# Flamingo gated block on one core: first batch's parts copied inside SBUF, masks written by VectorE, one transpose per kind and batch

## The reference

```
x = x + tanh(g_xattn) * xattn(layernorm(x), ctx)
x = x + tanh(g_ffn)   * moe(layernorm(x))

xattn: 16 heads of 8 channels
  y  = softmax(causal(q k^T / sqrt(8))) v          # self, q, k, v from x
  y += softmax(qc kc^T / sqrt(8)) vc               # cross, qc from x, kc, vc from ctx
  return y Wp + bp
moe: sigmoid router over 16 experts, best 2 of 4 groups, best 4 experts,
     out = sum_e combine[:, e] * (silu(x Wg_e) * (x Wu_e)) Wd_e
```

## Time and profile before

| what | value |
|---|---|
| median of three runs | 349.49 us |
| span of the profiled execution | 347.6 us |
| TensorE busy | 318.1 us (92%) |
| VectorE busy | 256.4 us (74%) |
| ScalarE busy | 196.2 us (56%) |
| GpSimd busy | 151.1 us (43%) |
| DMA, mean | 116 GB/s |
| bytes moved | 40.45 MB |

### The profile page before, as it was taken

One profiled execution on the slowest core, in us unless ns is written; L12 is line 12 of the kernel. 1 busy time (PEld: TensorE's weight loads), 2 busy tenths in 40 slices (PEclk: granted clock), 3 DMA queues, 4 the chain that ended last, 5 costly groups with the idle time before them and its releaser, 6 DMA issues.

```text
span 347.6 us, 8679 instructions
## 1 busy us (share of the span) xinstructions
PE 318.1 (92%) x3186; PEld 247.7 (71%) x3186; DVE 256.4 (74%) x639; ACT 196.2 (56%) x399; POOL 151.1 (43%) x176
## 2 busy tenths in 40 slices
PE   1579599989999999999999999999999999978696
PEld 0455365666687788778887888787888787856665
DVE  4238666868898888988798888888889854748742
ACT  2433356767667765687637765675666467532041
POOL 3884061404470588047633494318410722903422
PEclk9856759999999999999999999999999999989999
DMA  4269674688563855537655365077156005214000
GB/s 123 68 183 188 146 194 115 145 209 187 199 151 103 184 131 149 143 96 151 147 139 133 88 172 140 20 152 183 34 124 141 0 18 90 37 50 88 16 1 15
DMA packets 32889, 40.45 MB, mean 116 GB/s; under 512 B 3440, under 2 KB 29824, under 8 KB 30368
## 3 DMA queue, kind: packets, MB, share of 16 engines
q1 hardware_dynamic: 32004, 38.46, 46.7%
q10 hardware_dynamic: 844, 1.45, 1.7%
HBM read 29.84 MB, written 7.45 MB: 107 GB/s over the span
## 4 chain that ended last, share of the span: by engine, by line
PE 76%; DVE 7%; DMA 6%; SPq 5%; POOL 2%; issue 2%; ACT 1%; POOLq 0%; DVEq 0%
PE bank L918 15%; PE bank L846 14%; PE bank L825 8%; PE bank L943 7%; PE bank L800 7%; PE bank L803 6%; PE bank L822 5%; DMA k_stack<-tri_k 4%; SPq L427 2%; PE bank L893 2%; DVE row_max L1011 2%; PE bank L861 2%; PE bank L852 2%; SPq L426 1%; PE bank L956 1%
## 5 line engine op out<-in xcount | busy, mean ns | idle before, releaser
L1011 DVE TENSOR_REDUCE row_max<-bank 128x2 f32<-128x512 f32 (+1 forms) x224 | 146.9, 686 | 43.0 <-PE bank L803 24.9
L709 ACT ACTIVATE probs<-bank 128x512 f32<-128x512 f32 x224 | 127.5, 595 | 57.5 <-PE bank L825 27.7
L918 PE MATMUL bank<-xn2T,w_pairs_sb 128*128 128x256 f32 x256 | 68.0, 392 | 1.5 <-issue 0.9
L846 PE MATMUL bank<-probs,v_ext 128*32 128x256 f32 (+1 forms) x1024 | 57.2, 365 | 0.0
L626 POOL TENSOR_TENSOR f_h<-f_h,comb 128x512 f32<-128x512 f32 x32 | 40.3, 1273 | 36.1 <-DMA comb<-c_scr 20.4
L803 PE MATMUL bank<-k_stack,q_stack 72*128 72x256 bf16 x256 | 49.9, 284 | 2.7 <-DVE row_max L1011 2.1
L918 PEld LDWEIGHTS bank<-xn2T,w_pairs_sb 128*128 128x128 f32 x256 | 44.7, 193 | 8.3 <-issue 2.8
L825 PE MATMUL bank<-q_stack,k_stack 73*128 73x256 bf16 x256 | 49.2, 284 | 1.0 <-DMA q_stack<-shiftT 0.9
L412 POOL TENSOR_TENSOR rest<-proj,part 128x512 f32<-128x512 f32 x14 | 16.2, 1160 | 74.7 <-ACT part L682 74.6
L846 PEld LDWEIGHTS bank<-probs,v_ext 128*32 128x32 f32 x1024 | 30.0, 112 | 19.9 <-issue 4.7
L800 PE MATMUL bank<-k_stack,q_stack 121*128 121x128 bf16 (+1 forms) x384 | 39.1, 231 | 2.4 <-DMA k_stack<-tri_k 1.9
(11 more groups left out here) (113 smaller groups left out, 367.9 us busy)
## 6 DMA issues: line engine op xcount, KB each, us to landing
k_stack<-k_scr SPq DMA_DIRECT2D x45, 192.0 KB
q_stack<-q_scr SPq DMA_DIRECT2D x14, 576.0 KB
comb<-c_scr SPq DMA_DIRECT2D x14, 512.0 KB, 6.7
q_scr<-part SPq DMA_DIRECT2D x46, 64.0 KB
k_scr<-part SPq DMA_DIRECT2D x46, 64.0 KB
x_in<-in_x SPq DMA_DIRECT2D x8, 128.0 KB, 2.4
w_pairs_sb<-in_w_pairs SPq DMA_DIRECT2D x1, 1024.0 KB, 7.8
out<-y_out SPq DMA_DIRECT2D x8, 128.0 KB, 1.9
```

What stands on the lines that cost most here:

```text
L709: nc.scalar.activation(probs[:, seq % NP, :], exp_bank[s % 2][:, :], ACT.Exp).then_inc(exp_done, 1)
L846: last = pe.matmul(pv_bank[32 * n:32 * n + VW, col + q0:col + T], v[:, VW // 2 * odd:VW // 2 * odd + VW], weights, start=odd == 0 and kt = ...
L918: last = pe.matmul(bank_of[:, n * T:(n + 1) * T], w[:, e0:e0 + 128], xn2T[:, :], start=True, stop=True)
L1011: nc.vector.tensor_reduce(row_max[:, kind, qt, h0:h0 + nh], max_bank[k % 2][:, :].rearrange("p (h k) -> p h k", h=nh), AX.X, ALU.max).then ...
```

## The change

Batch 0 no longer goes through device memory. `copy_first` copies each part from SBUF into the stacks, 8 partitions of destination at a time: for each of the 2 kinds and 3 parts, three DMAs for q on SyncE's queue (`fq`) and three for k on ScalarE's (`fk`), 36 in all. ScalarE writes part 0 of batch 0 straight from PSUM, without `proj` (the query weights are multiplied by the scale once, beforehand, by VectorE), and VectorE takes the remainders of both kinds from PSUM (`first_rest`); GpSimd splits nothing of batch 0. The mask tiles are made at partitions 64 to 127 by GpSimd ahead of the first `rstd` (`masks:0`), with the shift row in them, and VectorE copies them into the stacks of all three slots (`tri`, six copies of 64 x 4096 bf16), two ahead of the splits of batch 0 and four ahead of the first reduction. The maxima and the router's weights are laid out so that one transpose gives all 256 tokens (rows are then heads times 2); the last batch's combT stays as it was. The waits for x and for the context are separate.

```diff
 'act':
-        xnT_e:0 proj_e:0 part0:0 pd0:0 proj_e:0:1 v_e:0 part0:0:1 qh:0 pd0:0:1 xnT_e:1 proj_e:1 part0:1 qh:0:1
-        proj_e:1:1 qst:0:1 part0:1:1 v_e:1 xnT_e:2 proj_e:2:1 sh_e:0 proj_e:2 sh_e:0:2 exp_e:0 exp_e:0:1 part0:2
+        xnT_e:0 proj_e:0 fk:0 proj_e:0:1 fk:0:1 fk:0:2 v_e:0 fk:0:3 fk:0:4 fk:0:5 xnT_e:1 proj_e:1 part0:1
+        proj_e:1:1 part0:1:1 v_e:1 xnT_e:2 proj_e:2:1 sh_e:0 proj_e:2 sh_e:0:2 exp_e:0 exp_e:0:1 part0:2
 'dve':
-        stats1:0 xnv:0 scale:0 stats1:1 sp1:0 sp3:0 stats1:2 tmax:0 ...
+        stats1:0 xnv:0 scale:0 gate:0 stats1:1 tri:0 tri:0:1 sp1:0 sp3:0 sp1:0:1 sp3:0:1 stats1:2 tri:0:2 tri:0:3 tri:0:4 tri:0:5 tmax:0 ...
 'pool':
-        rstd1:0 more:0 xres:0 rstd1:1 vclear:0 xn1:1 sp1:0:1 sp3:0:1 rstd1:2 ...
+        masks:0 rstd1:0 rows:0 xres:0 rstd1:1 xn1:1 vclear:0 rstd1:2 ...
 'sp':
-        load:0 w:0 load:1 load:2 ones:0 pd1:0 pd2:0 load:3 kh:0 pd1:0:1 pd2:0:1 kh:0:1 pd0:1 kst:0:1 tri:0 shd:0 pd2:1
-        pd1:1 pd1:1:1 pd0:1:1 pd2:1:1 shd:0:2 qst:1 kst:1 qst:1:1 shd:0:1 pd2:2 kst:1:1 tri:0:1 pd1:2 pd0:2 pd1:2:1
+        load:0 w:0 load:1 load:2 ones:0 fq:0 fq:0:1 fq:0:2 load:3 fq:0:3 fq:0:4 fq:0:5 pd0:1 pd2:1 pd1:1 shd:0
+        pd1:1:1 pd0:1:1 pd2:1:1 shd:0:2 qst:1 kst:1 qst:1:1 shd:0:1 pd2:2 kst:1:1 pd1:2 pd0:2 pd1:2:1
...
+        def first_rest(eng, kind):
+            src = (gate_bank, up_bank)[kind]
+            for at, bias in ((0, bias_q[:, 1 - kind:2 - kind]), (T, cols_sb[:, 3 - kind:4 - kind])):
+                last = eng.scalar_tensor_tensor(out=rest[:, kind, at:at + T], in0=src[:, at:at + T], scalar=bias,
+                                                in1=part[:, kind, 0, at:at + T], op0=ALU.add, op1=ALU.subtract)
+            last.then_inc(rest_done[kind], 1)
...
+        def copy_first(eng, qk, kind, n):
+            eng.wait_ge(split[kind], n + 1)
+            if kind == SELF:
+                eng.wait_ge(masks_in[0], 2)
+            src = part[:, kind, n, qk * T:(qk + 1) * T]
+            for i in range(PARTS):
+                if qk == 0:
+                    to = q_stack[n * BLOCK + i:(n + 1) * BLOCK:PARTS, 0, kind]
+                else:
+                    to = k_stack[i * BLOCK + n:(i + 1) * BLOCK:PARTS, 0, kind]
+                eng.dma_start(to, src).then_inc(part_out[kind][n], 16)
...
+        def place_masks(eng, qk, s):
+            eng.wait_ge(tri_made, 2)
+            st, tri = ((q_stack, tri_q), (k_stack, tri_k))[qk]
+            eng.tensor_copy(st[64:128, s, SELF], tri[64:128, 0:T].unsqueeze(1).broadcast_to([64, H, T])).then_inc(masks_in[s], 1)
...
-                heads = H // 2 if half else H
-                for m in range(NQ):
-                    last = pe.transpose(misc[0:heads, m * 128:(m + 1) * 128], row_max[:, n % 2, m, 0:heads], ident[:, :])
+                rows_out = (heads.stop - heads.start) * NQ
+                last = pe.transpose(misc[0:rows_out, 0:128], row_max[:, n % 2, heads, :].rearrange("p h m -> p (h m)"), ident[:, :])
```

More of the change, by code:

```diff
@@ L85 @@
 STACK_DMAS = (1 + PARTS, 2 + PARTS)
+FIRST_COPIES = 2 * PARTS
 GP = NB // 2
@@ L432, in load_rows, with load_stack @@
+        def load_stack(eng, b, kind, qk):
+            for n in range(PARTS):
+                eng.wait_ge(part_out[kind][n], stores_of_part(b))
+            ge(eng, exp_scores, (b - SLOTS) * NC2 + LAST_OF_KIND2[kind])
+            if kind == SELF and b < SLOTS:
+                eng.wait_ge(masks_in[b], 2)
+            src = (q_scr, k_scr)[qk][b % 2, kind].rearrange("p r h x -> (p r) h x").rearrange("r h x -> r (h x)")
+            here = stack_in[b % SLOTS][kind]
             if qk == 0:
                 src = src.unsqueeze(1).broadcast_to([BLOCK, PARTS, src.shape[1]])
-                eng.dma_start(q_stack[0:STACK, b % SLOTS, kind, heads], src).then_inc(signal, 16)
+                eng.dma_start(q_stack[0:STACK, b % SLOTS, kind], src).then_inc(here, 16)
+                if kind == SELF and b >= SLOTS:
+                    eng.dma_start(q_stack[SHIFT_ROW:SHIFT_ROW + 1, b % SLOTS, SELF], zero_row[:, :]).then_inc(here, 16)
@@ L435, in load_rows @@
             else:
                 for i in range(PARTS):
[L437 to L454, removed]
+                    eng.dma_start(k_stack[i * BLOCK:(i + 1) * BLOCK, b % SLOTS, kind], src).then_inc(here, 16)
+        def place_masks(eng, qk, s):
+            eng.wait_ge(tri_made, 2)
+            st, tri = ((q_stack, tri_q), (k_stack, tri_k))[qk]
+            eng.tensor_copy(st[64:128, s, SELF], tri[64:128, 0:T].unsqueeze(1).broadcast_to([64, H, T])).then_inc(masks_in[s], 1)
@@ L546, in _ @@
             sp.wait_ge(ones_in, 16 * SLOTS)
-            for s in range(SLOTS):
-                sp.wait_ge(tri_in[s], 32)
         @block.gpsimd
@@ L628, in _ @@
             for what, b, n in order("pool"):
-                if what == "more":
-                    more_constants()
+                if what == "masks":
+                    make_masks()
+                elif what == "rows":
+                    rows_of_constants()
                 elif what == "vclear":
```

201 lines of the change are left out of this document (111 added, 90 removed).

## The result

The change made no difference that 2% can tell, and within that it cost a little: 352.31 us in the median of 20 runs (349.43 to 360.0) against 350.53 us (346.58 to 354.74) of the kernel before in 20 runs beside it. The ratio is 1.006, with a 95% interval of 1.0031 to 1.0088. The ratios leave out executions in which the chip was in its slower state; the medians hold all. The profiled execution took 350.4 us, its span is 348.7 us, so it is 1.1 us longer than the span of before, and the forecast had it 1.4 shorter.

What follows compares the result with a forecast made beforehand. TensorE was taken to bound the kernel from 72 to 300 us (busy 226.7 of 228.0). Span 347.6 + 6.6 - 1.9 - 2.9 - 0.9 - 2.3 = 346.2 us, plus 1.9 to the median, said as 348 us; range 342 to 356.5.

Steps and rivals of the forecast that it cites:

- the start: Before the first score chunk: ScalarE's 18 copy issues of 0.65 us delay it by 6.6 us, to 29.8 us.
- the CROSS stretch: The 16 CROSS chunks after the first chunk: paced by VectorE, 15.1 us to the last shift, and that stays.
- The rival of cheap issues: ScalarE's queue: a copy inside SBUF is issued in 0.40 us, 4.5 us fall away, 343.6 us; chance 0.16.
- half width: Batch 0's 36 copies: 8-partition destinations use half the DMA engines, holding ScalarE to about 34 us; 356.3 us, chance 0.16.
- the mask wait and the shift wait: TensorE's idle time for the k mask goes, 1.9 us, and its wait for batch 1's shift, 0.9 us.
- the transposes: TensorE behind batch 0: 21 transposes fewer at 0.11 us each save 2.3 us.
- The rival in which they give nothing: Fewer transposes save nothing because TensorE's time is taken up by waits for VectorE: 350.4 us, chance 0.05.
- With it I expect the clock to hold: SELF chunks and first `pv`: without the mask's idle time they take 10.3 instead of 13.2 us, 2.9 less.
- Clock stays low: SELF chunks: short matmuls leave TensorE's clock at 0.50, the 2.9 us are not had, 351.0 us; chance 0.12.
- so I count nothing: Stack of batch 1: 9.7 us pass and its loads of 1.2 MB need 7.3, so no wait is booked.
- the mask copies: VectorE's copies of the masks into the stacks: 2.3 us each, 1.2 if they go by bytes.
- The rival of 4.4 us a copy: VectorE's mask copies run at 1.04 ns an element, VectorE is ready 17.3 us later, 358.8 us; chance 0.06.

Runs made afterwards that it cites:

- xnT_first: Changed kernel with ScalarE's list reordered, batch 1's transpose and first projection ahead of the nine SELF copies: 348.57 us, ratio to the kernel before 0.9919.
- t_only: Kernel before with only the transposes changed, one for each kind and batch: 346.93 us, ratio to the kernel before 0.9864.
- both: Changed kernel with the reorderings of `xnT_first` and `loads_early` together: 355.13 us, ratio to the kernel before 1.0193.
- mask_slot0: `t_masks` with VectorE writing only slot 0's masks and SyncE's queue copying the other slots by DMA: 345.73 us, ratio to the kernel before 0.9834.
- the fillers: 19 extra matmuls of 128 columns, results unread, behind chunks: 354.29 us in the kernel before, 357.01 us in the changed kernel.
- warm_after: Changed kernel with 19 filler matmuls of 128 columns behind chunks, results unread: 357.01 us, ratio to the kernel before 1.0233.
- t_masks: Kernel before with one transpose per kind and batch and VectorE's six mask copies, batch 0 still through device memory: 346.69 us, ratio to the kernel before 0.9855.
- loads_early: Changed kernel with SyncE's list reordered, CROSS stack loads of batches 1 and 2 moved earlier: 358.08 us, ratio to the kernel before 1.0292.

## Why the prediction was right or wrong

It said 348 us and a range of 342 to 356.5, no change by 2% being likeliest. The time is in the range and the class is that one, but the sign was wrong: 1.8 us above before in place of 1.5 below. The span came 2.5 us above the forecast one (348.7 against 346.2), and the table has where: 2.1 us for the clock and 1.3 for the two stacks, then 0.7 for the last stretch and 0.4 for the start, against 1.75 the other way in the CROSS stretch and 0.3 for the waits that went. The step from span to time held: every launch on record is 1.7 to 1.8 us above its own span, where 1.9 was added.

**Right: the start.** The sum had 29.8 us for the first chunk, by issues of 0.65 us; it came at 30.20. The median issue on ScalarE's queue was 0.71 us with SyncE issuing beside it, and the three of part 0 took 2.94 us together. `xnT_e:1` waited for them, which `xnT_first` shows by moving it. The rival of cheap issues (0.40 us) is refuted. Its 343.6 was also mis-added: the first three copies would only have waited for part 1, due at 15.3 us, so 15 of the 18 issues save time and not all, 344.4 us. And of the chance of 0.15 for less than 342.5 us, a third of this rival makes 0.05; the rest was not worked out.

**Right: half width, but not the rival.** The DMA engines' slices from 12 to 30 us stand mostly at 5 to 6 tenths with both queues at work, at a mean of 125 GB/s, the load of batch 3 included. That is what the Trainium skill's rule (DMA: Bandwidth & Descriptors, Why a DMA increments its semaphore by 16 and not by 1) would have for destinations of 8 partitions, and the trace agrees. But the longest issue was 1.48 us and the median 0.71, so the issuing engine was never held until the copies had landed, and the 356.3 us of this rival did not come.

**Right: the mask wait and the shift wait.** For the mask 1.9 us were forecast and 2.05 measured up to the first SELF chunk; for the shift of batch 1 0.9 were forecast and 1.04 measured, up to 73.41 us.

**Right in kind, short in size: the transposes.** 2.3 us were forecast. From 80 us on the changed kernel gains 1.8 up to 300 us and 1.6 up to the end of the span, at a place where the kernel with two transposes gains nothing up to 300 us. The rival in which they give nothing is refuted for this stretch. That `t_only` gains 4.1 us in the medians and not 2.3 isn't explained, and neither is the last batch, behind 300 us.

**Wrong, and it cost the sign: "With it I expect the clock to hold".** The step took the 1.92 us of idle before the SELF chunks for what lowers the clock behind them, and booked 2.9 us. Without the wait the stretch ran at 0.58 instead of 0.51 and gave 0.8 us. `both` and `mask_slot0`, with no mask wait either, run it at 0.52 and 0.51. The wait and the low clock stood side by side in one trace; taking away the one did not take away the other. What sets the clock there stays open, the fillers being the one hint. The size was about right: at full clock the stretch takes 10.3 us in `warm_after`, fillers included. This is the rival "Clock stays low", at 351.0 us and a chance of 0.12; the profiled execution took 350.4. (The rival without a gain from the transposes has 350.4 itself, by a mechanism that the runs speak against.)

**Wrong: the stack of batch 1, "so I count nothing".** The stacks of batches 1 and 2 were late, with waits of 0.54 us at 56.53 and 0.53 at 80.49, and the two stretches up to them lost 1.3 us where nothing had been booked. Without this miss alone, as without the clock's alone, the span would have been no longer than that of before. The margin that was worked out (9.7 us between issue and need, 7.3 for the bytes) left out the issues themselves: the shift row, q and k take from 46.24 to 48.8 us, and the last load then lands 7.69 us later. The batch 2 stack was in no term.

**Unforecast: the CROSS stretch.** It was said to stay at VectorE's pace and was 1.75 us shorter, at a clock of 0.97 where before had this:

```profile
23.10:38.30 15.20, 12.60 (x55) 7.06 (x53) 12.67 (x23) 4.67 (x12) 6.13 (x6) 0.69 0.89 184
```

Part of TensorE's time in it was on the path before. That was luck: it hid half of the two misses above, and `both`, which starts this stretch earlier, has it at 0.71 and 16.5 us.

**Mis-sized, with no effect: the mask copies.** 2.3 us were taken and 1.22 to 1.24 came. The 1.2 us that the prediction named for a copy by bytes was the right one. The Trainium skill (VectorE: DVE Perf Modes, The perf-mode tier table) has bf16 copies within SBUF at four elements a cycle, about 1.2 us by the prediction's estimate; the trace agrees with it. The rival of 4.4 us a copy is refuted. What no term held was the other engine: GpSimd's small passes took up to 2.3 us instead of 0.2 to 0.7 while VectorE copied.

## What to carry to other kernels

A transfer that is replaced by many small ones costs its issuing engine some 0.7 us each, and whatever stands behind them in that engine's list is late by the sum: put the next batch's first step ahead of all copies that are not yet needed (here worth 1.4%). Before booking a gain in clock, ask whether the stretch itself, with its short matmuls, might keep it low, at which the two profiles with fillers hint: an idle gap that stands beside the fall need not be its cause. And when a load has a margin, count the issues on its queue as well as its bytes, and what small transfer would stand behind it if it moved.

## What the runs showed of the hardware

- A bf16 copy inside SBUF of 64 partitions by 4096 elements took VectorE 1.22 to 1.24 us in the changed kernel, 0.30 ns an element, against 0.53 ns by the one-source passes.
- While VectorE does such copies, GpSimd's passes stretch: 3.01 instead of 1.50 us for 512 elements, 2.19 instead of 0.71 for two. The copies stretch as well: beside GpSimd's splits in `t_masks` four of them took 1.30, 1.63, 1.62 and 2.17 us.
- A copy inside SBUF onto 8 partitions of destination was issued in 0.71 us at the median on ScalarE's queue and 0.67 on SyncE's (0.62 and 0.64 in `xnT_first`). While 36 of them moved, the queues together moved 125 GB/s.
- The shift rows issued from 46 to 83 us landed 1.8 to 3.3 us after their issue in the changed kernel, and up to 7.0 us with stack loads issued ahead of them (`loads_early`).
- The 53 matmul records of the CROSS stretch kept TensorE busy for 9.0 of 13.0 us at a granted clock of 1.00 (`mask_slot0`) and for 14.8 of 18.4 us at 0.50 (`t_masks`), though VectorE is the busier engine at the full clock (12.2 us of the 13.0).
